# A cross-attention kernel: the second key half moved directly behind the second turns, value tiles behind the value products or ahead of those turns, and the copy of the probabilities split in two

## What is computed

```python
# x: 64x512, ctx: 6272x512
q = (layernorm(x) @ Wq + bq)            # 64 x 32 heads x 128
k, v = split(ctx @ Wkv + bkv)           # 6272 x 8 heads x 128 each
o = softmax(q @ k.T / sqrt(128)) @ v    # 4 query heads share one k/v head
x = x + o @ Wo + bo
x = x + attn_and_gated_layers(x)        # weights NF4[codes] * scales, plus low rank
x = x + linear_with_fourier_adapter(x)
```

## Time and profile before

| | |
|---|---|
| median of three executions | 1011.46 us (1010.75 to 1011.51) |
| the profiled execution | 1011.92 us |
| its span, first to last instruction | 1010.1 us |
| granted TensorE clock | 1.0 (2.4 GHz) over the span |
| busy: TensorE / VectorE / ScalarE / GpSimd | 99 / 74 / 58 / 44% |
| share of TensorE in the chain that ended last | 93% |

### The profile page before, as it was taken

The page is one execution under the profiler, slowest core; times in us unless marked ns, Lnnn a source line. Parts: engine busy times, 40 slices in busy tenths (PEclk is TensorE's granted clock), DMA queues, the critical chain, the costliest instruction groups (busy, mean ns, idle before and its releaser), DMA issues.

```text
span 1010.1 us, 20355 instructions
## 1 busy us (share of the span) xinstructions
PE 995.1 (99%) x7083; PEld 921.6 (91%) x7083; DVE 745.5 (74%) x1680; ACT 586.5 (58%) x1254; POOL 443.5 (44%) x641
## 2 busy tenths in 40 slices
PE   8999999999999999999999999999999999999998
PEld 6779999999999999999999999999999999999744
DVE  5678878777777778777776778777777768676766
ACT  6466666666565656566565666656565655565431
POOL 2244553545534444345454444534444445333331
PEclk9999999999999999999999999999999999999999
DMA  9663333333324343243333334333333237464895
GB/s 324 226 223 130 124 129 132 109 134 108 124 94 134 119 135 135 96 134 108 131 106 116 114 132 137 116 119 108 130 107 134 97 124 249 158 223 153 235 351 166
DMA packets 90086, 149.59 MB, mean 148 GB/s; under 512 B 10529, under 2 KB 44977, under 8 KB 89985
## 3 DMA queue, kind: packets, MB, share of 16 engines
q1 hardware_dynamic: 88224, 146.42, 43.8%
q10 hardware_dynamic: 1424, 1.51, 0.4%
q0 software_dynamic: 336, 0.35, 0.2%
HBM read 82.97 MB, written 14.81 MB: 97 GB/s over the span
## 4 chain that ended last, share of the span: by engine, by line
PE 93%; DVE 3%; DMA 2%; issue 1%; SPq 0%; ACT 0%; DVEq 0%
PE p_kv L88 16%; PE p_kv L90 16%; PE p_kv L89 16%; PE p_s L88 7%; PE p_s L90 7%; PE p_s L89 6%; PE p_t L769 6%; PE p_o L88 5%; PE p_o L90 5%; PE p_o L89 5%; PE p_s L849 1%; PE p_ot L753 1%; DMA wkv_raw<-in_wkv 1%; PE p_o L783 1%; DMA probs_r<-probs 1%
## 5 line engine op out<-in xcount | busy, mean ns | idle before, releaser
L610 POOL TENSOR_SCALAR slots<-code 128x512 f32<-128x512 bf16 x232 | 148.7, 641 | 247.3 <-DVE slots L1466 162.4
L1210 ACT ACTIVATE pt_hi<-p_t 128x512 fp32r<-128x512 f32 x224 | 109.9, 542 | 113.6 <-PE p_t L769 107.9
L1466 DVE TENSOR_TENSOR slots<-slots 128x512 f32<-128x512 f32 x232 | 170.0, 733 | 1.6 <-POOL slots L610 1.5
L1239 ACT ACTIVATE slots<-code,drop_and_offsets 128x512 f32<-128x512 bf16 x232 | 158.6, 713 | 8.1 <-POOL code L606 4.1
L1198 ACT ACTIVATE v_hi<-p_kv 128x256 fp32r<-128x256 f32 x196 | 75.2, 384 | 139.6 <-PE p_kv L90 138.7
L630 POOL TENSOR_TENSOR slots<-slots 128x512 f32<-128x512 f32 x58 | 77.0, 1327 | 158.2 <-DVE slots L1466 158.2
L1430 DVE TENSOR_TENSOR pt_lo<-p_t,pt_hi 128x512 fp32r<-128x512 f32 x224 | 128.7, 614 | 5.9 <-ACT pt_hi L1210 4.9
L1415 DVE TENSOR_TENSOR v_lo<-p_kv,v_hi 128x256 fp32r<-128x256 f32 x196 | 83.1, 424 | 67.6 <-ACT v_hi L1198 64.8
L88 PE MATMUL p_kv<-wkv_hi,ctx_even_hi 128*128 128x256 f32 x448 | 129.1, 288 | 0.2 <-DVE v_lo L1415 0.2
L89 PE MATMUL p_kv<-wkv_lo,ctx_even_hi 128*128 128x256 f32 x448 | 126.0, 281 | 0.0
L90 PE MATMUL p_kv<-wkv_hi,ctx_even_lo 128*128 128x256 f32 x448 | 126.0, 281 | 0.0
(11 more groups left out here) (261 smaller groups left out, 2717.7 us busy)
## 6 DMA issues: line engine op xcount, KB each, us to landing
probs_r<-probs SPq DMA_DIRECT2D x110, 448.0 KB, 3.6
code<-in_codes SPq DMA_DIRECT2D x58, 256.0 KB, 3.8
scale<-in_scales SPq DMA_DIRECT2D x114, 128.0 KB, 3.1
expanded_weights<-slots SPq DMA_DIRECT2D x56, 256.0 KB, 2.1
ctx_st<-in_ctx_t SPq DMA_DIRECT2D x96, 112.0 KB, 3.0
ring_hi<-expanded_weights SPq DMA_DIRECT2D x22, 256.0 KB, 5.9
ring_lo<-expanded_weights SPq DMA_DIRECT2D x22, 256.0 KB, 6.0
wq_hi<-in_wq SPq DMA_DIRECT2D x4, 1024.0 KB, 7.2
```

The costliest lines, as they stand in the source:

```text
L610: nc.gpsimd.tensor_scalar(slots[:, slot, :], code16[:], LINES[j][0], LINES[j][1], ALU.mult, ALU.add).then_inc(pool_lines, 1)
L1210: nc.scalar.activation(pt_hi[:, at:at + n, :].rearrange("p t q -> p (t q)"), p_t[:, c % 2, 0:n * ROWS], ACT.Copy).then_inc(pt_rounded, 1)
L1239: nc.scalar.activation(slots[:, slot, :], code16[:], ACT.Identity, bias=offsets[:, k:k + 1], scale=LINES[j][0]).then_inc(act_lines, 1)
L1466: nc.vector.tensor_tensor(slots[:, slot, :], slots[:, slot, :], slots[:, other, :], ALU.max).then_inc(merged, 1)
```

## The change

TensorE: key half 1 now stands directly behind the second turns in every block. In an even block the value tiles move behind the value product of tiles 4 to 6, so they end the block. In an odd block they move in front of the second turns, behind the first value product. Block 54 makes its seven tiles in one go. The banks of the tiles, the numbers in `kv_number` and the waits follow: the second score half now waits for whatever was last in the previous block (`last_kv`). VectorE's, ScalarE's and GpSimd's orders are rewritten to go with it. The copy of the probabilities becomes a front part (tiles 0 to 3, 512 columns), which only waits for the first turns, and a back part (384 columns), which waits for the second turns. Context places and pieces are moved (place 2 is rounded in the odd block and place 4 in the next even one), and key half 0 of head 0 waits for the context piece by piece. GpSimd's two first lines of a tile are separated by a context split.

```diff
     elif pair == 0:
-        piece = (0, 1, PIECES, PIECES, 2)[place]
+        piece = (0, 1, PIECES, 2, 3)[place]
+    elif pair == 1 and place < 2:
+        piece = (4, PIECES)[place]
...
+        FRONT, BACK = slice(0, PT_TILES * P), slice(PT_TILES * P, CHUNK)
...
             def move_probs(i):
 
                 if i > 0:
+                    sp.wait_ge(pt_psum, 4 * i - 2)
+                for r in range(RT):
+                    sp.wait_ge(exp_ready, 2 * i + 1 + r)
+                    sp.dma_start(probs_r[:, r, FRONT].bitcast(F32), probs[:, r, FRONT]).then_inc(front_moved, 16)
+                if i > 0:
                     sp.wait_ge(pt_psum, 4 * i)
                 for r in range(RT):
-                    sp.wait_ge(exp_ready, 2 * i + 1 + r)
-                    sp.dma_start(probs_r[:, r].bitcast(F32), probs[:, r]).then_inc(probs_moved, 16)
+                    sp.dma_start(probs_r[:, r, BACK].bitcast(F32), probs[:, r, BACK]).then_inc(back_moved, 16)
...
# TensorE, block_work
+                if i == 3:
+                    turn_output(0)
                 turn_probs(i - 1, 0)
                 turn_probs(i - 1, 1)
...
                 next_keys(i, h, half, 0)
                 weigh_values(i - 1, 0, SPLIT_TILE)
                 if i == 2:
                     query_product(7)
+                if i % 2 == 1:
+                    for t in value_tiles(i):
+                        value_tile(i, h, half, t)
                 turn_probs(i - 1, 2)
                 turn_probs(i - 1, 3)
                 if i > 2:
                     turn_output(i - 2)
-                if s == 0 and h % 2 == 0:
-                    pe.wait_ge(wkv_split, wkv_turn(h + 1) + 1)
-                for t in value_tiles(i)[:SPLIT_TILE]:
-                    if i == 2 and t == 2:
-                        query_turn(7)
-                    value_tile(i, h, half, t)
                 next_keys(i, h, half, 1)
                 if i == 1:
                     query_product(6)
                 weigh_values(i - 1, SPLIT_TILE, CT)
-                if i == 2:
-                    turn_output(0)
-                for t in value_tiles(i)[SPLIT_TILE:]:
-                    value_tile(i, h, half, t)
+                if i % 2 == 0:
+                    if s == 0:
+                        pe.wait_ge(wkv_split, wkv_turn(h + 1) + 1)
+                    for t in value_tiles(i):
+                        if i == 2 and t == 2:
+                            query_turn(7)
+                        value_tile(i, h, half, t)
...
# VectorE, block_work, the part of an even block behind the second probability splits
+                if h % 2 == 0:
+                    merge(i, 2)
                 split_keys(i, h, 1)
...
+                else:
+                    for t in value_tiles(i):
+                        split_values(i, t)
+                        if t < 3:
+                            merge(i, 3 + t)
+                        if t == 1 and i < NKV - 2:
+                            split_wkv(h + 2)
+                        if t == 2 and i == 2:
+                            finish_query(7)
```

More of the change, by code:

```diff
@@ L1315, in block_work @@
                 if h % 2 == 0:
-                    round_ctx(s, h, half, 0)
+                    lines(i, 3, 4)
                 if i == 2:
                     query_out(7)
+                if h % 2 == 1:
+                    for t in value_tiles(i):
+                        round_values(i, t)
+                        if t == SPLIT_TILE + 1 and 1 < i < NKV - 2:
+                            round_wkv(h + 2)
                 round_probs(i - 1, 2)
                 round_probs(i - 1, 3)
+                round_ctx(s, h, half, 0 if h % 2 == 0 else 3)
@@ L1335, in block_work @@
[L1335 to L1342 removed]
+                    query_out(6)
+                    lines(i + 1, 0, 2)
+                if h % 2 == 0:
+                    for t in value_tiles(i):
+                        round_values(i, t)
+                        if t == 0 and i < NKV - 2:
+                            round_wkv(h + 2)
+                        if t == 1:
+                            if i >= NKV - 2:
+                                lines(i + 1, 0, 1)
+                            round_ctx(s, h, half, 1)
+                        if t == 2:
+                            lines(i + 1, 0 if i < NKV - 2 else 1, 2)
@@ L1620, in block_work @@
                 split_keys(i, h, 0)
-                merge(i, 2)
-                split_probs(i - 1, 2)
-                split_probs(i - 1, 3)
-                if i == 1:
-                    split_wkv(3)
+                if h % 2 == 1:
+                    tiles = value_tiles(i)
+                    for n in range(CT - SPLIT_TILE):
+                        if tiles:
+                            split_values(i, tiles[n])
+                        if n == 0:
+                            merge(i, 2)
+                        elif n == 1:
+                            merge(i, 3)
+                            merge(i, 4)
+                    split_probs(i - 1, 2)
+                    split_probs(i - 1, 3)
+                    if 1 < i < NKV - 2:
+                        split_wkv(h + 2)
+                    else:
+                        merge(i, 5)
+                else:
+                    split_probs(i - 1, 2)
+                    split_probs(i - 1, 3)
                 if i == 6:
```

111 lines of the change are left out of this document (54 added, 57 removed).

## The result

The changed kernel took 1014.77 us, the median of six executions (1013.79 to 1017.28); the kernel before, beside it, 1011.49 us (1010.07 to 1012.81). The ratio is 1.0036, with a 95% interval of 1.0025 to 1.0047. The change costs 3.3 us by the medians and 3.6 by the ratio, and the forecast of 1011.1 us (1008.5 to 1014.0) missed it. In six of the fourteen traces of this document, one of them of the old order (e8_split_alone), the granted clock falls in the first block, to a mean of 0.72 between 18 and 24 us, and that block takes 1.5 to 2.2 us longer; so block 0 is left out where traces are compared.

A forecast was written before the change was run, and what follows sets the result against it. TensorE's own work was taken as the bound, so order wins only where it idles or restarts. The terms -0.8+0+1.7+0.2-1.6+0.4-0.3 gave -0.4 us on the median of 1011.46: 1011.1 us, range 1008.5 to 1014.0.

The forecast's parts named there:

- Part 4: Start-up, blocks 1 and 2: the two-part copy and moved loads remove most of TensorE's idle time; -1.6 us.
- the 1.95 us idle: TensorE's idle time from 62.0 to 70.3 us in the profile before, of which 1.1 to 1.95 us was to go.
- Part 3: End of block 2: VectorE's query step and wkv split delay tile 3's split, +1.7 us; block 4 about +0.2.
- Part 2: Value tiles last in even blocks: the first score half just covers the last tile's split; 0, up to 0.1 us a block.
- rival (B): Even blocks' last value tile lacks cover, so the second score half waits; 1013.8 to 1016.5 us, chance 0.15.
- Part 1: Key half 1 directly behind the second turns: restart costs 0.06 instead of 0.08 us in some 54 blocks; -0.8 us.
- Parts 5 and 6: Block 7 waits once for a late context piece, +0.4 us; block 50 loses its value split wait, -0.3 us.
- Rival (C): Late context pieces or merges waiting for GpSimd's lines cost 0.1 us on 54 blocks, +5.4, 1016.5 us; chance 0.07.
- Part 4's 0: Steady blocks: the back copy leaves later in odd blocks but lands within 5.4 us of cover; cost 0.

The follow-up runs named there:

- e8_split_alone: The kernel before the change with only the copy of the probabilities split into front and back part; 1011.96 us, ratio 1.0006 to before.
- e2_wkv3_later: The changed kernel with VectorE's split of wkv piece 3 moved from the end of block 1 to behind block 2's second probability splits; one execution, block 2 19.30 us.
- e10_two_merges: The changed kernel with one VectorE merge per even block from block 8 moved from behind value tile 1's split to behind tile 2's; one execution, 1019.13 us.
- e11_query_alone: The changed kernel with head 7's query turned right behind block 2's second turns and finished before key half 1's split; 1013.28 us, ratio 1.0022 to before.
- e7_one_copy: The changed kernel with wkv piece 3 and head 7's query both behind block 2's second turns, and the probabilities copied in one part again; 1014.76 us, ratio 1.0035.
- e9_best: The changed kernel with wkv piece 3, head 7's query, block 4's wkv piece and context piece 2 moved to other places in the start-up; 1010.53 us, ratio 0.9987.

## Why the prediction was wrong

**Part 4 failed, by the most.** The step was "Of the 1.95 us idle, between 1.1 (the back part lands as late as before) and 1.95 goes". Measured against the two profiles of before, blocks 1 and 2 together changed by -0.22 and by +0.93 us instead of -1.6. The copy did land earlier, the loads behind it did move. But I followed ScalarE's queue to its end and not VectorE's: the split of `wkv` piece 3 now ends block 1, between the split of key half 1 and the statistics, and the join holds it for 1.1 us. It costs block 2 about 2.0 us (e2_wkv3_later beside e10_two_merges), and the late context piece up to 0.8 us more; the latter the prediction saw and left out of its sum. Without both, block 2 falls to 19.30 us. The second fault is that the term stood on the idle time of one execution. The prediction noted that this execution was above the median and drew nothing from it.

**Part 3 was right in place and mechanism, and too small.** The split of tile 3 was to end 3.0 us behind the start of the scores; it ended at 3.05. Block 3 +2.14 us (forecast +1.7, at most +2.0), block 5 +0.63 us (+0.2). VectorE's queue was as worked out, and GpSimd lay over the query. It held the cast, not the last subtraction. Block 5 needed a second overlap that I didn't look for, GpSimd's context split over the `wkv` split (1.69 us). The query edit of e11_query_alone takes block 3 from 17.74 to 15.92 us, which shows the cause.

**Part 2 was right:** 0 in the steady blocks, rival (B) absent, and e10_two_merges shows that the cover is thin, as argued.

**Part 1 was wrong by 0.8 us.** It took 0.06 against 0.08 us from two pairs of rounded rows and put the difference down to the width of the matmul. It belongs to the place: about 0.07 us behind the first turns and 0.085 behind the second, where 448 columns cost what 256 did. Blocks 8 to 49 differ by 0.05 us in all.

**Parts 5 and 6** were right: block 7 +0.29 us (forecast +0.4), block 50 -0.47 us (-0.3).

In the sum, -0.4, + 0.8 for Part 1, + 0.9 for what Part 3 lacked, - 0.3 for Parts 5 and 6 and + 1.4 or + 2.5 for Part 4 is 2.4 or 3.5 us; the span grew by 2.6 us against the one profile of before and by 3.5 against the other. Parts 1 and 3 alone would have turned the sign. Rival (C) came in its mechanism and not in its price: VectorE's merges wait 0.5 us each for GpSimd's lines in the steady blocks, and TensorE for none of it. So the sign that the prediction gave for (C), VectorE waiting for GpSimd's lines, was too weak; only a wait of TensorE would have told. The rival that ended on this side was missing from my list: work with no deadline of its own in front of the statistics. Part 4's 0 for the later back copy in the steady blocks held; with a single copy three of those blocks lose 0.8 to 0.9 us each (e7_one_copy).

## What to carry to other kernels

When a stall is to be removed, follow every engine's queue from there to the next thing that TensorE needs, with the work that was moved in it, and ask what stands in front; here TensorE's next wait changed its name from a copy to a split. Work without a deadline belongs where its engine idles in the trace (e9_best), not at the end of a block, where it stands in front of the next block's first step. Take a second profile before a term rests on a start-up stall. Where VectorE and GpSimd work on SBUF at the same time, price each VectorE step that reads only SBUF twice, alone and held; the Trainium skill, page "SBUF — State Buffer", section "Who interferes with whom", says that copies and casts can take the shared ports as well as operations with two SBUF inputs, and the cast of 0.29 us that took 1.17 us under the join agrees.

## What the hardware showed unexpectedly

A cast with a single SBUF input, 128x256, took 0.29 us free and 1.17 or 1.18 us under GpSimd's join; I had expected that only for operations with two inputs. GpSimd is held in turn: its multiplication (L648) behind the join at 63.97 us took 2.04 us beside the split of `wkv` piece 3, and 1.26 us behind another join (in e2_wkv3_later). TensorE's idle 2.83 us in e2_wkv3_later was followed, about a microsecond behind its restart, by some 3 us at a lower granted clock, down to 0.50; the 1.7 us of idle time in the changed kernel at the same place was not. And a program whose engines' orders are fixed doesn't repeat its start-up exactly: blocks 1 and 2 of the kernel before took 36.18 and 35.03 us in its two traces, in which a context piece landed at 66.4 and 65.4 us, and block 2 of the changed order 22.06 us, and 21.33 in e10_two_merges.
